# Writing out the loops over batches and over pairs of attention groups on every engine

## The chip, the cores and the metric

The kernel runs on one core of one Trainium2 chip. The metric is the device time of one execution in microseconds (us). Its engines are PE (matrix products; PEld is its weight load), DVE (vector), ACT (scalar), POOL (general) and SP, which here only issues transfers. Each runs its own list of instructions; they meet at semaphores.

## The reference, cut to what matters

Two transformer layers on x of (2, 1024, 1024), all in fp32: attention with rotary positions, a mixing layer, attention again, and an expert layer. The change touches the two attentions alone:

```python
x = x + _L0_attn_ref(_layernorm(x), wq, wk, wv, wo)   # 32 heads of 32, 8 key/value heads
x = x + _L0_ffn_ref(_layernorm(x), ...)
x = x + _L1_attn_ref(_layernorm(x), Wq, Wk, Wv, Wo)
x = x + _L1_ffn_ref(_layernorm(x), ...)

# in each attention, for batch b and key/value group g (4 query heads each):
scores = q @ k.T / sqrt(32), causal mask
attn = softmax(scores)
out = attn @ v
```

## The kernel before, in words

`attention` is built once for each layer. On every engine it has the same skeleton: some work for the first batch, then `batches` runs a function `batch` for the 2 batches, and inside it, after a prologue (the first projections), `over_groups` runs a function `group` for the 8 key/value groups. Groups 0 to 5 are three passes of a loop that executes on the engine (`eng.Fori`, L318) with two groups in its body, an even and an odd one; groups 6 and 7 are written out. `batches` has a loop too (L311), with a single pass for batch 0, while batch 1 is written out behind it. So there are 2 layers x 2 batches = 4 group loops on each engine, each with 3 passes and 2 taken branches back; "pair" below is one pass.

What a group does is set by hand in `ORDER` (`ORDER_7` for group 7), one list for all engines. `ST:e.h` is the transposed score product of unit e and head h on PE (L898), whose exponential ACT takes (L617). `S` are row scores of the next group (PE L851), whose maxima DVE takes (L710 with the mask, L713 without). `V` and `D` are the products with the values and with ones (L914, L927). `P:c.i` are pieces of the projection of a later group (L830), 24 products for one of two halves c. `MT` takes the larger of the two halves of the maxima (DVE L719), transposes them (PE L860) and sends them on. `NORM` is the division by the sum (DVE L758 to L764). `WS` prepares the weights of the next projection: ACT L590 takes the high part, POOL L463 the low one. Group 6 has the same list as 0 to 5 but for the projections (`P`, `WL`, `WS`, `RK`, `VG` and some more).

PE has a PSUM ring of three banks for `S` and `P` and another of three for `ST`; it waits for DVE (`sh_free`) or ACT (`exp_done`) until a bank is free again. Such a wait compares a semaphore, which only counts up, with a number like `SH0 + u + prev + 1`, where u depends on the batch and on the group. In the loop of L318 the group's number is in a register. So most waits in the loop's body compare with a register, and an instruction of the engine's own sequencer (REGISTER_ALU, or ISA, in the order below; ALU_OP or FUSED_REGOPS in a trace) computes it first. The batch's loop has one pass, and what depends on b is a constant already. Groups 6 and 7 and the prologue have constants throughout.

Of the kernel before, what the change touches and what calls it, by code (L numbers as in the profile page):

```python
# [22 lines left out]
B, S, D = 2, 1024, 1024  # L23
# [5 lines left out]
NG = 8  # L29
# [184 lines left out]
def attention(nc, sem, layer, x_in, wqkv, cos_in, sin_in, swap, oT_d):  # L214
# [37 lines left out]
    with ExitStack() as ctx:  # L252
# [55 lines left out]

        def batches(eng, batch):

            with eng.Fori(0, B - 1) as b:  # L311
                batch(b, False)
            batch(B - 1, True)

        def over_groups(b, eng, group, last):

            u0 = 1 + b * U_BATCH + U_PRO
            with eng.Fori(0, NG // 2 - 1) as j:  # L318
                for par in range(2):
                    group(bodies[par], b, j * 2 + par, j, par, u0 + (j * 2 + par) * U_IT)  # L320
            group(body6, b, NG - 2, NG // 2 - 1, 0, u0 + 6 * U_IT)
            group(body7 if last else ahead7, b, NG - 1, NG // 2 - 1, 1, u0 + 6 * U_IT + U_IT6)

        @block.sync
        def _(sp):
# [89 lines left out]
            def batch(b, last):  # L415

                sp.wait_ge(s["zT_ready"], ZT0 + (b + 1) * 2 * ST_)
                sp.sem_inc(s["sp_turn"], 1)
                def keys_and_queries(g):

                    if g == 0:
                        sp.wait_ge(s["k_out"], b * 64 + 32)
                        sp.sem_inc(s["sp_turn"], 1)
                        sp.wait_ge(s["st_ready"], ST0 + b * NG * NU * GH)
                        sp.sem_inc(s["sp_turn"], 1)
                    stack_keys(b, g, g)
                    for c in range(2 - g):
                        sp.wait_ge(s["q_lo"], b * RB + 2 * LO_ORDER.index((1, 4)[g]) + c + 1)
                        stack_queries(b * 2 * NG + g * 2 + c, g, c)

                load_w(b * N_WCHUNK + 2, 2, 0)
                store_k(b, 0)
                load_w(b * N_WCHUNK + 3, 3, 1)
                keys_and_queries(0)
                load_w(b * N_WCHUNK + 4, 4, 0)
                store_k(b, 1)
                load_w(b * N_WCHUNK + 5, 5, 1)
                load_w(b * N_WCHUNK + 6, 6, 0)
                keys_and_queries(1)
                load_w(b * N_WCHUNK + 7, 7, 1)  # L440
                sp.wait_ge(s["k_out"], b * 64 + 64)
                sp.sem_inc(s["sp_turn"], 1)
                row_max(b, 0, 0)
                over_groups(b, sp, group, last)

            batches(sp, batch)
            for qc in range(NQC):
                sp.wait_ge(o_stored[qc], DMA0 + 16 * B * NG)
# [5 lines left out]
        def _(pool):  # L454
# [98 lines left out]
            def batch(b, last):  # L553
                w_lo(b * N_WCHUNK + 1, 1)
                for step in pro:
                    what, p, *piece = step
                    if what == "P" and piece[1] == PIECES - 1:
                        c = piece[0]
                        i, _, _ = plan_pro[step[:-1]]
                        u = 1 + b * U_BATCH + i  # L560
                        if c == 0:
                            w_lo(b * N_WCHUNK + p + 1, (p + 1) % 2)
                        if p in VALUES:
                            pool.wait_ge(s["sh_free"], SH0 + u + 1)
                            pool.sem_inc(s["pool_turn"], 1)
                            pool.drain().then_inc(s["roped"], 1)
                        else:
                            turn_over(u, c)
                        if p in (1, 4) and c == 0:
                            part_lo(b * RB + 2 * LO_ORDER.index(p), 0)  # L570
                        if c == 1 and p in (0, 1, 2):
                            for h in range(p % 2, 2):
                                part_lo(b * RB + 2 * LO_ORDER.index(p) + h, h)
                    if what == "VT" and piece == [1]:
                        pool.wait_ge(s["v_ready"], b * 4 + 2 + 2 * VALUES.index(p))
                        pool.sem_inc(s["pool_turn"], 1)
                        if p == VALUES[0]:
                            copy_v(b, 0, 0)
                            copy_v(b, 1, 1)
                over_groups(b, pool, group, last)  # L580

            batches(pool, batch)

        @block.scalar
        def _(act):
# [66 lines left out]
            def batch(b, last):  # L652
                for p in range(6):
                    w_hi(b * N_WCHUNK + p + 1, b * 6 + (p + 1) // 2, (p + 1) % 2)
                    if p == 1:
                        act.wait_ge(s["k_out"], b * 64 + 32)
                    if p == 4:
                        act.wait_ge(s["k_out"], b * 64 + 64)
                    if p not in VALUES:
                        for c in range(2 if p < 4 else 1):  # L660
                            if p == 2:
                                act.wait_ge(s["q_out"], (b * 2 * NG + c + 1) * 32)
                            part_hi(b * N_WCHUNK + p, c)
                over_groups(b, act, group, last)

            batches(act, batch)

        @block.vector
# [1410 lines left out]
```

## Time and profile before

| | us |
|---|---|
| three timed runs | 2863.57, 2864.22, 2868.37 |
| median | 2864.22 |
| the profiled execution, its own time | 2866.59 |
| its span, first to last instruction | 2864.9 |
| PE busy | 2603.4 (91%) |
| DVE busy | 1780.9 (62%) |
| POOL busy | 1125.1 (39%) |
| ACT busy | 1094.2 (38%) |
| granted clock of PE, mean | 0.958 |

The profiled execution lies 2.37 us over the median, and 1.69 us of its own time lie outside its span. The two attentions take the stretches from the start to about 940 us and from about 1435 to 2390 us. The rest is the mixing layer between them, and the output projection and the expert layer at the end; those have loops of their own, which stay. Busy times of PE are modelled ends, since products overlap; an idle time counts only where the waits show one. Register, branch and semaphore instructions aren't counted as busy. In the views a lower-case q behind an engine's name stands for its sequencer, and "issue" as releaser is idle time for which the profile shows no one that was waited for.

### The profile page before, as it was taken

To read this page: it belongs to the slowest core of one execution; us is meant where nothing else is said; L and a number is where in the kernel's file an instruction comes from. 1 tells how busy PE (TensorE), PEld (TensorE's weight loads), DVE (VectorE), ACT (ScalarE), POOL (GpSimd) and SP (SyncE) were. 2 spreads that over 40 slices of the span, in tenths; PEclk is the share of its full clock that TensorE was granted. 3 is DMA by queue.
4 is the path that set the end of the run, shared out by engine and by line. 5 is a ranking of instruction groups with operands and counts; after the bars stand their busy time and mean duration, and the time that the engine had idled before them with its cause. 6 is when DMAs were issued, how large, how long until landed. Compare 5 with 4: busy or idle time off the path is not lost. (4 is left out here: it accounts for less than half of the span.)

```text
span 2864.9 us, 50928 instructions
## 1 busy us (share of the span) xinstructions
PE 2603.4 (91%) x15312; PEld 1826.8 (64%) x15312; DVE 1780.9 (62%) x4439; ACT 1094.2 (38%) x2381; POOL 1125.1 (39%) x801
## 2 busy tenths in 40 slices
PE   7999997999998799793979999989999996998999
PEld 6665654765654588682757566547656544886887
DVE  5677777567775433588756777775667763216443
ACT  2255454155555211372522454551454553002000
POOL 7466554556564100000063666546555642002110
PEclk9999999999999899896979999999999998999999
DMA  4323222432321421000243232224222314461211
GB/s 157 116 72 102 75 72 82 133 92 75 98 74 39 163 81 59 1 1 0 108 159 118 70 108 67 80 71 143 85 76 90 83 40 153 134 241 38 74 59 45
DMA packets 121076, 252.97 MB, mean 88 GB/s; under 512 B 12720, under 2 KB 39728, under 8 KB 120880
## 3 DMA queue, kind: packets, MB, share of 16 engines
q1 hardware_dynamic: 120912, 251.03, 27.4%
q8 instruction: 72, 1.18, 0.2%
q14 instruction: 92, 0.75, 0.1%
HBM read 166.57 MB, written 84.41 MB: 88 GB/s over the span
## 5 line engine op out<-in xcount | busy, mean ns | idle before, releaser
L617 ACT ACTIVATE a_prob<-a_pst 128x512 f32<-128x512 f32 (+3 forms) x1536 | 660.4, 494 | 535.5 <-PE a_pst L898 529.5
L710 DVE CUSTOM_DVE_ANT_0 a_psh<-a_psh,a_edge 128x128 f32<-128x128 f32 (+3 forms) x1024 | 480.0, 516 | 203.6 <-PE a_psh L851 182.7
L898 PE MATMUL a_pst<-a_qst,a_kst 128*128 128x512 f32 (+2 forms) x1536 | 487.6, 370 | 24.1 <-DMA a_qst<-rowmax 17.7
L517 POOL TENSOR_TENSOR a_prob<-a_prob 128x2048 f32<-128x2048 f32 (+1 forms) x96 | 405.9, 4228 | 245.6 <-PE a_ppv L914 230.0
L851 PE MATMUL a_psh<-a_kst,a_qst 127*128 127x512 f32 (+3 forms) x1536 | 485.3, 364 | 16.7 <-DVE a_mx L710 10.6
L851 PEld LDWEIGHTS a_psh<-a_kst,a_qst 127*128 127x128 f32 x1536 | 273.1, 190 | 230.7 <-DVE a_mx L713 92.7
L713 DVE TENSOR_REDUCE a_mx<-a_psh 128x1 f32<-128x512 f32 x512 | 329.1, 685 | 122.0 <-PE a_psh L851 120.9
L898 PEld LDWEIGHTS a_pst<-a_qst,a_kst 128*128 128x128 f32 x1536 | 286.2, 193 | 163.7 <-ACT a_prob L617 92.8
L914 PE MATMUL a_ppv<-a_prob,a_vg 128*32 128x512 f32 (+3 forms) x3072 | 321.8, 505 | 0.0
L502 POOL TENSOR_SCALAR_AFFINE_SELECT a_prob<-a_prob 128x512 f32<-128x512 f32 x256 | 162.2, 641 | 186.5 <-ACT a_prob L617 186.5
L927 PE MATMUL a_pden<-a_prob,a_ones 128*32 128x512 f32 (+3 forms) x2304 | 221.3, 474 | 9.0 <-POOL a_prob L517 9.0
L470 POOL TENSOR_TENSOR a_swp<-a_swp,a_sin 128x512 f32<-128x512 f32 x80 | 103.3, 1292 | 246.4 <-DVE a_swp L699 235.5
L830 PE MATMUL a_psh<-a_xT_hi,a_w_hi 128*128 128x512 f32 x416 | 170.7, 410 | 8.2 <-DVE a_vall L803 6.6
L1538 PE MATMUL h_pout<-h_w,h_o 128*128 128x512 f32 x720 | 167.7, 392 | 0.3 <-DVE h_x L1404 0.3
L830 PE MATMUL a_psh<-a_xT_hi,a_w_lo 128*128 128x512 f32 x416 | 165.5, 398 | 0.0
L830 PE MATMUL a_psh<-a_xT_lo,a_w_hi 128*128 128x512 f32 x416 | 165.1, 397 | 0.0
L1538 PEld LDWEIGHTS h_pout<-h_w,h_o 128*128 128x128 f32 x720 | 134.0, 188 | 28.2 <-issue 0.7
L830 PE MATMUL a_pst<-a_xT_hi,a_w_hi 128*128 128x512 f32 x352 | 139.6, 397 | 6.2 <-DVE a_swp L780 3.2
L710 DVE DVE_READ_ACCUMULATOR2_ANT a_mx<- 128x1 f32 x1024 | 143.0, 140 | 0.0
L914 PEld LDWEIGHTS a_ppv<-a_prob,a_vg 128*32 128x32 f32 x3072 | 71.9, 109 | 110.8 <-issue 66.4
L830 PE MATMUL a_pst<-a_xT_lo,a_w_hi 128*128 128x512 f32 x352 | 137.8, 392 | 0.0
L830 PE MATMUL a_pst<-a_xT_hi,a_w_lo 128*128 128x512 f32 x352 | 137.6, 391 | 0.0
(239 smaller groups left out, 4190.6 us busy)
## 6 DMA issues: line engine op xcount, KB each, us to landing
a_qst<-q SPq DMA_DIRECT2D x192, 256.0 KB, 4.4
a_wraw<-in_wqkv SPq DMA_DIRECT2D x52, 512.0 KB, 4.3
q<-a_stg_hi SPq DMA_DIRECT2D x64, 256.0 KB, 2.1
q<-a_stg_lo SPq DMA_DIRECT2D x64, 256.0 KB, 2.4
a_kst<-kT SPq DMA_DIRECT2D x96, 128.0 KB, 2.5
oT<-a_oT SPq DMA_DIRECT2D x32, 256.0 KB, 2.4
oT<-a_vT SPq DMA_DIRECT2D x32, 256.0 KB, 2.9
h_oraw<-oT SPq DMA_DIRECT2D x16, 512.0 KB, 4.0
```

The source lines that it names most:

```text
L470: pool.tensor_tensor(swp[c][:, :], swp[c][:, :], sin[:, c * BANK:(c + 1) * BANK], ALU.mult)
L502: pool.affine_select(out=blk, in_=blk, compare_op=ALU.is_ge, fill=0.0, base=0, pattern=[[0, GH], [1, P]], channel_multiplier=-1)\
L517: pool.tensor_tensor(into, into, prob[second % len(prob)][:, :, off:], ALU.add)\
L617: act.activation(prob[k % len(prob)][:, h, off:], pst[:, (k * GH + h) % 3, off:], ACT.Exp, scale=scale).then_inc(s["exp_done"], 1)
L710: part = dve.tensor_tensor_reduce(scores, scores, edge[:, BANK - n:], 1.0, 2 * MASKED, ALU.add, ALU.max, mx_hq[kc][:, h, qt:qt + 1])
L713: part = dve.tensor_reduce(mx_hq[kc][:, heads[0]:heads[0] + m, qt], psh[:, at, 0:m * n].rearrange("p (m n) -> p m n", n=n), AX.X, ALU.max)
L830: mm = pe.matmul(bank(at), w[par][a][:, k, :], xT[x][:, k, c * BANK:(c + 1) * BANK], start=(i == 0), stop=(i == len(passes) - 1))
L851: mm = pe.matmul(psh[:, at, i * n:(i + 1) * n], qst[par][0:P - 1, h, qt * P:(qt + 1) * P], kst[par][0:P - 1, kc * BANK:kc * BANK + n], sta ...
L898: pe.matmul(pst[:, (k * GH + h) % 3, off:], kst[par][:, ki * P:(ki + 1) * P], qst[par][:, h, qc * BANK + off:(qc + 1) * BANK], start=True, ...
L914: mm = pe.matmul(ppv[h * HD:(h + 1) * HD, off:], vg[par][:, ki, :], prob[k % len(prob)][:, h, off:], start=(ki == 0), stop=(ki == 4 * qc + ...
L927: mm = pe.matmul(pden[h * HD:(h + 1) * HD, off:], ones[:, :], prob[k[0] % len(prob)][:, h, off:], start=(ki == 0), stop=(UNITS[k[-1]][1] = ...
L1538: mm = pe.matmul(pout[:, half, :], o[:, par, a, k, :], w[:, b, k, half * BANK:(half + 1) * BANK], start=(i == 0), stop=(i == len(passes) - 1))
```

## The change

Both loops become loops of the program that builds the kernel, and each engine gets its passes written out one behind the other. `batches` calls `batch` for 0 and 1 and `over_groups` calls `group` for 0 to 5 with plain numbers. So in the two attentions the branches go, and so do the instructions that compute a wait's number or a transfer's address from a register. Every other instruction stays, in its order.

```diff
--- before.py
+++ after.py
@@ -308,14 +308,13 @@
 
         def batches(eng, batch):
 
-            with eng.Fori(0, B - 1) as b:
-                batch(b, False)
-            batch(B - 1, True)
+            for b in range(B):
+                batch(b, b == B - 1)
 
         def over_groups(b, eng, group, last):
 
             u0 = 1 + b * U_BATCH + U_PRO
-            with eng.Fori(0, NG // 2 - 1) as j:
+            for j in range(NG // 2 - 1):
                 for par in range(2):
                     group(bodies[par], b, j * 2 + par, j, par, u0 + (j * 2 + par) * U_IT)
             group(body6, b, NG - 2, NG // 2 - 1, 0, u0 + 6 * U_IT)
```

On DVE, this is how the loop of layer 0, batch 0 begins; its first row stands once ahead of the three passes, the second is the first of the body. ISA rows of L710 are a masked maximum and the reading of its result; L318 is the loop.

```order
L318 UNCONDITIONAL_BRANCH
L318 ISA
L710 ISA a_psh,a_mx<-a_psh,a_edge 128x128
L710 ISA a_mx 128x1
```

And this is how that body ends on DVE: the last projection's rotation, the division of the odd group, the branch.

```order
L694 REGISTER_ALU
L697 REGISTER_ALU
L698 TENSOR_TENSOR a_rots<-a_psh,a_cos 128x512
L699 STREAM_SHUFFLE a_swp<-a_psh 128x512
L755 REGISTER_ALU
L758 STREAM_TRANSPOSE a_vT<-a_dens 128x512
L760 RECIPROCAL a_rden<-a_vT 128x16
L762 STREAM_TRANSPOSE a_dens<-a_rden 128x512
L764 TENSOR_TENSOR a_vT<-a_pvs,a_dens 128x512
L318 REGISTER_ALU
L318 COMPARE_AND_BRANCH
```

In the changed kernel the same place on DVE, between groups 1 and 2, reads as follows (its lines stand one lower).

```order
L697 TENSOR_TENSOR a_rots<-a_psh,a_cos 128x512
L698 STREAM_SHUFFLE a_swp<-a_psh 128x512
L757 STREAM_TRANSPOSE a_vT<-a_dens 128x512
L759 RECIPROCAL a_rden<-a_vT 128x16
L761 STREAM_TRANSPOSE a_dens<-a_rden 128x512
L763 TENSOR_TENSOR a_vT<-a_pvs,a_dens 128x512
L709 ISA a_psh,a_mx<-a_psh,a_edge 128x128
L709 ISA a_mx 128x1
```

The maxima of group 2 now stand directly behind the division of group 1: the branch is gone, and so are the rows that computed numbers. Nothing else moved.

On ACT the start of the loop's body, in layer 0, batch 0, has one computed number for nearly every exponential.

```order
L318 ISA
L616 ISA
L617 ACTIVATE a_prob<-a_pst 128x512
L616 REGISTER_ALU
L617 ACTIVATE a_prob<-a_pst 128x512
L616 REGISTER_ALU
```

In the changed kernel ACT has there, at the same place, only the exponentials and the high part of the projection between them.

```order
L616 ACTIVATE a_prob<-a_pst 128x512 x4
L616 ACTIVATE a_prob<-a_pst 128x384 x3
L601 ACTIVATE a_stg_hi<-a_rots 128x512
L616 ACTIVATE a_prob<-a_pst 128x384
```

The work is the same and in the same order; the rows between it are gone.

## Rows read from the trace of the kernel before

**Rows 1.** page, part 1: engine, busy us (share) xinstructions.
```profile
span 2864.9 us, 50928 instructions
PE 2603.4 (91%) x15312; PEld 1826.8 (64%) x15312; DVE 1780.9 (62%) x4439; ACT 1094.2 (38%) x2381; POOL 1125.1 (39%) x801
```

**Rows 2.** busy time by stretch: us, PE, PEld, DVE, ACT, POOL, clock, DMA.
```profile
204.45:298.72 94.27, 92.38 (x626) 56.68 (x627) 70.57 (x192) 49.65 (x110) 56.83 (x38) 1.00 0.30 87
298.72:393.19 94.47, 92.45 (x627) 56.69 (x628) 70.57 (x192) 49.64 (x110) 56.82 (x38) 1.00 0.31 87
668.95:763.47 94.52, 92.35 (x627) 56.67 (x628) 70.56 (x192) 49.66 (x110) 56.80 (x38) 1.00 0.30 87
763.47:857.95 94.48, 92.35 (x626) 56.69 (x627) 70.54 (x192) 49.65 (x110) 56.80 (x38) 1.00 0.30 87
1642.80:1736.28 93.48, 92.13 (x626) 56.73 (x627) 70.50 (x192) 49.64 (x110) 56.83 (x38) 1.00 0.30 88
1736.28:1829.80 93.52, 92.19 (x626) 56.75 (x627) 70.49 (x192) 49.64 (x110) 56.84 (x38) 1.00 0.29 88
2102.85:2202.68 99.83, 94.80 (x627) 57.90 (x628) 70.78 (x192) 49.75 (x110) 56.85 (x38) 0.97 0.29 82
2202.68:2301.41 98.73, 93.91 (x626) 57.17 (x627) 70.69 (x192) 49.73 (x110) 56.85 (x38) 0.98 0.29 83
```

**Rows 3.** timeline, PE, 1736 to 1736.5: start, us, operation.
```profile
1736.28 0.28 PE L860 MATMUL a_psh<-a_ident,a_mx 128*32 128x128 f32 x1 [0.56 <-DVE a_mx L719]
```

**Rows 4.** waits: us in total, times, longest.
```profile
DVE a_psh L710 <- issue: 18.1, 8, 3.0
PE a_psh L860 <- DVE a_mx L719: 16.0, 28, 0.9
PE a_psh L851 <- DVE a_mx L710: 10.6, 6, 3.8
```

**Rows 5.** timeline, DVE, 2109.5 to 2122.
```profile
2110.34 1.18 DVE L764 TENSOR_TENSOR a_vT<-a_pvs,a_dens 128x512 f32<-128x512 f32 x1
2113.54 0.30 DVE L710 CUSTOM_DVE_ANT_0 a_psh<-a_psh,a_edge 128x128 f32<-128x128 f32 x1 [2.02 <-issue]
...
2117.36 0.30 DVE L710 CUSTOM_DVE_ANT_0 a_psh<-a_psh,a_edge 128x128 f32<-128x128 f32 x1 [2.96 <-issue]
```

**Rows 6.** timeline, DVE, 1650.2 to 1655.
```profile
1650.29 1.18 DVE L764 TENSOR_TENSOR a_vT<-a_pvs,a_dens 128x512 f32<-128x512 f32 x1
1651.39 0.29 DVE L710 CUSTOM_DVE_ANT_0 a_psh<-a_psh,a_edge 128x128 f32<-128x128 f32 x1
```

**Rows 7.** timeline, PE, 2111 to 2123.
```profile
2117.77 0.80 PE L851 MATMUL a_psh<-a_kst,a_qst 127*128 127x256 f32 x2 [3.81 <-DVE a_mx L710]
```

**Rows 8.** busy time by stretch, the two at half clock.
```profile
2116.20:2123.00 6.80, 5.23 (x21) 3.05 (x25) 3.91 (x15) 0.94 (x3) 1.45 (x2) 0.50 0.70 193
2218.60:2222.00 3.40, 3.40 (x17) 1.34 (x19) 2.30 (x9) 0.94 (x3) 1.27 (x1) 0.50 0.85 198
```

**Rows 9.** busy time by stretch: ST:8.0 to ST:10.3 in groups 1 and 6.
```profile
1627.28:1635.22 7.94, 7.94 (x47) 4.14 (x46) 6.11 (x15) 4.39 (x11) 5.32 (x4) 1.00 0.02 4
1860.26:1868.20 7.94, 7.94 (x47) 4.14 (x46) 6.11 (x15) 4.39 (x11) 5.24 (x4) 1.00 0.00 0
```

**Rows 10.** timeline, DVE and POOL, before the maxima's transposition.
```profile
1828.08 1.59 DVE L719 TENSOR_TENSOR a_mx<-a_mx 128x16 f32<-128x16 f32 x1 [0.18 <-issue]
...
1827.27 2.37 POOL L463 TENSOR_TENSOR a_w_lo<-a_wraw,a_w_hi 128x1024 fp32r<-128x1024 f32 x1 [0.35 <-ACT a_w_hi L590]
...
1872.69 0.17 DVE L719 TENSOR_TENSOR a_mx<-a_mx 128x16 f32<-128x16 f32 x1
```

**Rows 11.** DMA queues, 115.84 to 204.45: packets, MB, share of 16 engines.
```profile
q8 instruction: 6, 0.10, 0.5%
```

**Rows 12.** busy time by stretch, first ST to the transposition.
```profile
115.84:204.45 88.61, 87.24 (x605) 52.69 (x604) 63.85 (x180) 48.57 (x108) 53.50 (x35) 1.00 0.28 82
1647.75:1736.28 88.53, 87.19 (x605) 52.66 (x604) 66.74 (x185) 48.56 (x108) 56.83 (x38) 1.00 0.31 91
```

## The prediction, made before the changed kernel ran

> **What bounds the kernel now.** I first read the page's busy times: PE is busy for 91% of the span, the next engine, DVE, for 62% [rows 1]. Averages over stages with different limits prove little, so the second view is the busy time by stretch, cut at one mark that returns with every pair of groups: the transposition of the maxima on PE (L860), the last thing before the branch [rows 3]. There are eight such stretches, two behind each of the four group loops [rows 2]. Each holds the same 626 or 627 products, so they can be compared with each other. The reader should see three kinds. The two pairs of layer 1, batch 0 take 93.48 and 93.52 us, with PE busy 92.13 and 92.19 at a clock of 1.00: PE's own work bounds them. The four pairs of layer 0 take 94.27 to 94.52, at the same clock. The two of layer 1, batch 1 take 99.83 and 98.73, at 0.97 and 0.98. The same code on the same shapes should not take three different times.
>
> The third view, the waits, names the difference [rows 4]. PE waited 10.6 us in 6 waits for the masked maxima of DVE (L710), and DVE stood idle before those maxima for 18.1 us in 8 gaps which the profile puts down to "issue": it waited for nobody. Eight stretches, six of them long, and six waits of PE: they belong together. The timeline shows where. In the first pair of the last loop DVE's division L764 starts at 2110.34 and lasts 1.18 us, and the next maximum, the first thing behind the branch back, starts at 2113.54; after three more maxima comes a second hole of 2.96 us, until 2117.36 [rows 5]. In layer 1, batch 0, at the same place, the maximum starts 1.10 us after the division does, 1651.39 against 1650.29, and there is no hole [rows 6]. So a taken branch costs DVE some 2 to 3 us of its time in six cases of eight, and in two of these the code behind it stops DVE a second time. I read it as DVE fetching its instructions again: the body is long, and where its pieces lie in the instruction memory is another in each of the four copies. PE has little in reserve at this point, since its PSUM ring is three banks deep. [...]
>
> **The change part by part.** It removes from the attentions all taken branches (8 on each engine), and the instructions that compute numbers for waits and addresses. It adds no work, wait or queue entry and moves none past another; it adds only code that has to be fetched.
>
> *The branches.* The reference is the mean of the two undisturbed pairs, (93.48 + 93.52) / 2 = 93.50 [rows 2]. Layer 0: 94.27 + 94.47 + 94.52 + 94.48 = 377.74, less 4 x 93.50 = 374.00, is 3.74 us. Layer 1, batch 1: 99.83 + 98.73 = 198.56, less 187.00, is 11.56 us. This second sum can be split by the same rows: the idle time of PE is 5.03 and 4.82 there against 1.34 in a clean pair, together 7.17 more, and the busy time is 94.80 and 93.91 against 92.16, together 4.39 more, which is the half clock. In layer 1, batch 0 nothing is to be had. Sum: 15.30 us. When the hole goes, what is late next is nothing new: a clean pair already runs with 1.33 to 1.35 us of idle PE.
>
> [...]
>
> *The computed numbers.* They are cheap to bound, because group 6 runs the same list with constants. From product ST:8.0 to ST:10.3, a stretch without projections in both, group 1 (registers) takes 7.94 us and group 6 (constants) 7.94 us, with PE busy throughout [rows 9]. So they hide behind PE's work and I take zero. The upper end: the one wait of PE that remains in a pair is for the transposition, 16.0 us in 28 waits [rows 4], 24 of them in the loops at 0.56 [rows 3], 13.4 us. It would be gained only if DVE's L719 came earlier. But L719 lasts 1.59 us in the loop and 0.17 in group 6; it starts at 1828.08, 0.81 us behind the weight preparation of POOL, which runs from 1827.27 to 1829.64, and ends with it, at 1829.67 [rows 10]. One computed number fewer ahead of it is part of a gap of 0.18 us; it would have to be 0.81 earlier. POOL's start hangs on ACT and so on PE. I take zero, and keep 13.4 as the end of the gain. A loss from fewer instructions I bound at zero too, but for the fetching below.
>
> *The longer code.* Today the second and third pass fetch nothing on PE; the first pass does, 6 packets of code [rows 11]. With everything written out all passes fetch like the first. The first pass of layer 0, batch 0, from its first ST to the transposition, takes 88.61 us; the second of layer 1, batch 0, with its code in place, takes 88.53 [rows 12]. So straight code streams in at a price of 0.08 us at most per pass. Eight passes become such: 0.6 us, within what two equal passes differ by; I take zero. The other end: a late fetch is worth as much as a branch today, and the rival below counts it. No gap of DVE before L710 lies elsewhere: six branches and the two second holes make up all eight [rows 4].
>
> Stages outside the attentions keep their code and their loops. Their code lies elsewhere in memory, but loops with much shorter bodies show no such idle time in the waits, so I expect no change there.
>
> **The sum.** 2866.59, the profiled execution's own time, less 15.30 is 2851.3. It stood 2.37 us over the median of the runs, so for the median I say 2864.2 - 15.3 = 2848.9, about 2849 us.
>
> **The rivals.**
> *The computed numbers matter too.* Each engine's sequencer has less to do, DVE answers earlier, and the wait at the transposition shrinks. For it speaks that nearly every wait in the loop has one such instruction in front; against it the equal 7.94 [rows 9]. With half of 13.4 it is 2842, with all of it 2835.5.
> *The half clock stays.* PE's clock may fall at these places for another reason than the hole, and only the idle time goes. Then of 15.3 the 4.4 of the slow products stay: 2853.3. For it speaks that other stretches without a hole fall too, since the mean is 0.958; against it that in the loops both falls stand right behind the two longest stalls of PE, and the six cleaner pairs have 1.00 [rows 2, 8].
> *The holes move and the end doesn't.* If DVE's hole only takes time that PE then loses at the transposition, the time is that of before, 2864. Against it: the clean pairs have the same wait there, 0.56 [rows 3], and are shorter.
> *Straight code arrives late: slower.* Place: PE, at each new piece of its code, in the eight passes that fetch none today. At the first pass's rate of 6 that is 48 pieces. Price: a packet keeps a DMA engine busy for 0.005 x 16 x 88.6 / 6 = 1.2 us [rows 11], and a piece that comes too late holds PE for at least that; all 48 make 57 us, so 2906. It decides from 13 late pieces on, where it eats the 15.3. Against it stands the first pass, which fetched 6 and lost 0.08 [rows 12].
> That the change doesn't do what it says is excluded: in the order of the changed kernel the branches and the computed numbers are gone.
>
> **How the numbers follow.** The forecast as worked out (2845 to 2853) gets 0.70, the first rival 0.10, the second 0.11, the third 0.05, the fourth 0.04. What a measurement of this kernel can tell from no change is about 0.2%, 5.7 us: faster means below 2858.5, slower above 2869.9. The forecast and the first two rivals lie below; the third is the same; the fourth is mostly slower. That gives faster 0.90, same 0.06, slower 0.04. For the range I take the forecast's own bounds and go down to 2840, which holds the half of the first rival, and up to 2857, which holds the second rival and a run like the slowest of the three, 4 us over the median.
>
> **What the changed profile would show.** Right: "DVE L710 <- issue" and "PE L851 <- DVE L710" all but gone; every pair from transposition to transposition at 93.5 us, in layer 1, batch 1 too, at a clock of 1.00; PE's wait at the transposition unchanged at 0.56; more packets of code on the queue that PE's come by. Wrong: pairs well under 93.4 would show that the computed numbers cost something; a pair that stays above 94 without a gap on DVE, that the holes were not the cause; gaps with the releaser "issue" on PE or DVE in the middle of a group, that straight code comes late.

## The result, and the profile after

The written-out kernel takes 2850.95 us (median of 5 runs, 2849.54 to 2854.61), the kernel before 2867.75 in the same comparison: ratio 0.9946, 95% interval 0.9936 to 0.9957. Forecast were 2849.0 us and a gain of 15.3; the medians differ by 16.8, the profiled executions (2866.59 and 2849.54) by 17.05. The size is right. The places are right only in part, as the stretches show. Lines of the kernel after are one lower than before: L859 is the transposition of the maxima (L860 before), L850 the row scores, L709 the masked maxima.

The page after, parts 1 and 3, and its line of code packets in the kernel before below it:

```profile
span 2847.4 us, 44980 instructions
PE 2593.4 (91%) x15312; PEld 1821.4 (64%) x15312; DVE 1783.5 (63%) x4439; ACT 1093.3 (38%) x2381; POOL 1123.5 (39%) x801
q8 instruction: 108, 1.77, 0.3%
q14 instruction: 86, 0.70, 0.1%
```

```profile
q8 instruction: 72, 1.18, 0.2%
q14 instruction: 92, 0.75, 0.1%
```

PE is busy 10.0 us less than in [rows 1] with the same 15312 products. The mean granted clock is 0.964 over the span, where the kernel before had 0.958; since the clock is either 1.00 or 0.50, that is 206 us of 2847.4 at half speed against 242 of 2864.9. 5948 instructions fewer ran (44980 against 50928), and queue 8 has 36 packets more, 108 against 72. I call queue 8 that of PE's code, since its count follows PE's loops alone: 108 in all five kernels of this study with PE written out, 72 in the nine others. Queue 14 follows the other engines: 92 packets before, 92 with PE alone written out, 86 with all but PE, 76 with DVE alone.

After, the eight pairs of groups from transposition to transposition, as in [rows 2], and the first of the two stretches over group 6 in layer 0, then that of layer 1 (columns as in [rows 2]):

```profile
202.87:296.21 93.34, 92.08 (x626) 56.75 (x626) 70.89 (x192) 49.62 (x110) 56.72 (x38) 1.00 0.30 89
296.21:389.83 93.62, 92.07 (x627) 56.74 (x628) 70.80 (x192) 49.69 (x110) 56.73 (x38) 1.00 0.30 89
666.06:760.52 94.46, 92.13 (x627) 56.75 (x627) 70.98 (x192) 49.72 (x110) 56.75 (x38) 1.00 0.30 88
760.52:854.19 93.67, 92.32 (x627) 56.74 (x628) 70.44 (x192) 49.61 (x110) 56.71 (x38) 1.00 0.30 89
1636.84:1730.35 93.51, 92.06 (x627) 56.74 (x628) 70.85 (x192) 49.62 (x110) 56.71 (x38) 1.00 0.31 89
1730.35:1823.77 93.42, 92.03 (x626) 56.74 (x627) 70.80 (x192) 49.61 (x110) 56.71 (x38) 1.00 0.31 89
2096.86:2191.00 94.14, 92.14 (x626) 56.73 (x626) 70.91 (x192) 49.61 (x110) 56.72 (x38) 1.00 0.31 88
2191.00:2284.34 93.34, 92.09 (x627) 56.76 (x628) 70.82 (x192) 49.53 (x110) 56.74 (x38) 1.00 0.30 89
389.83:436.39 46.56, 42.34 (x280) 23.17 (x281) 32.39 (x93) 23.15 (x53) 22.07 (x15) 0.96 0.14 41
1823.77:1867.06 43.29, 40.95 (x281) 22.51 (x281) 32.20 (x93) 23.05 (x53) 22.06 (x15) 1.00 0.15 44
```

The kernel before at the two group-6 stretches of layer 0:

```profile
393.19:437.08 43.89, 42.55 (x280) 23.03 (x281) 32.12 (x93) 23.20 (x53) 22.07 (x15) 0.96 0.15 44
857.95:901.35 43.40, 40.97 (x281) 22.52 (x281) 32.12 (x93) 23.16 (x53) 22.07 (x15) 1.00 0.15 44
```

The eight pairs now add up to 749.50 us, against 763.30 in [rows 2]: 13.80 less. Every clock is 1.00. But group 6 of layer 0 is longer, 46.56 against 43.89, and in batch 1 (854.19 to 900.48) 46.29 against 43.40: 5.56 us given back. As a result the last instruction of layer 0's attention starts at 945.0 us, where it started at 944.75 before: nothing is left of its gain. The attention of layer 1, from DVE's first instruction in it to the start of the last one, went from 948.5 to 934.7 us. The sum of all is 17.5 us of span: +0.25 up to the end of layer 0's attention, -3.33 in the mixing stage, -13.75 in layer 1's attention, -0.67 behind it.

The waits after, with the one of before that answers to the last row below them (columns as in [rows 4]):

```profile
PE a_psh L859 <- DVE a_mx L718: 13.7, 28, 0.6
PE a_psh L850 <- DMA a_qst<-q: 12.7, 16, 2.8
```

```profile
PE a_psh L851 <- DMA a_qst<-q: 3.5, 7, 1.3
```

Both waits of DVE's holes are gone from the list, "DVE L710 <- issue" (18.1) and "PE L851 <- DVE L710" (10.6) of [rows 4]. The timeline of DVE after, at the branch's old place in layer 1, batch 1, against [rows 5]:

```profile
2104.18 1.25 DVE L763 TENSOR_TENSOR a_vT<-a_pvs,a_dens 128x512 f32<-128x512 f32 x1
2105.35 0.29 DVE L709 CUSTOM_DVE_ANT_0 a_psh<-a_psh,a_edge 128x128 f32<-128x128 f32 x1
```

The maximum starts 1.17 us after the division, as in [rows 6], where it was 3.20 in [rows 5]. What took their place is a wait for a transfer: PE at the row scores (L850) for the second half of the next group's queries, 12.7 us in 16 waits. The longest is in group 6 of layer 0:

```profile
411.60 0.79 PE L850 MATMUL a_psh<-a_kst,a_qst 127*128 127x512 f32 x1 [2.80 <-DMA a_qst<-q]
```

SyncE's queue shows why it is late. First the kernel before, group 6 of layer 0, batch 0: two stores of the queries' parts, then the three transfers that stack them.

```profile
404.54 0.33 SPq L342 DMA_DIRECT2D q<-a_stg_hi  x1
404.92 0.43 SPq L342 DMA_DIRECT2D q<-a_stg_lo  x1
407.31 1.28 SPq L345 DMA_DIRECT2D a_qst<-q  x3
```

And after:

```profile
401.09 0.33 SPq L341 DMA_DIRECT2D q<-a_stg_hi  x1
401.46 0.43 SPq L341 DMA_DIRECT2D q<-a_stg_lo  x1
405.88 1.56 SPq L344 DMA_DIRECT2D a_qst<-q  x3
```

The stacking waits for the stores to land. From the second store it took 2.39 us before and takes 4.42 after. The DMA view of these few microseconds (KB each, median us from issue to landing) follows, first before (403 to 410), where it has no line of queue 8, as no packet of that queue starts between 201.2 and 411.9, then after (400.5 to 409), where it has one:

```profile
q<-a_stg_lo SPq DMA_DIRECT2D x1, 256.0 KB, 2.4
```

```profile
q8 instruction: 1, 0.02, 0.7%
q<-a_stg_lo SPq DMA_DIRECT2D x1, 256.0 KB, 4.4
```

A packet of PE's code, 16384 bytes in 0.96 us, starts at 403.4, while the store is under way, and the store lands 2.0 us later than it did before. PE then waits 2.80 us, and its clock is at half from 411.3 to 414.7 (0.96 over the stretch). The kernel before has a half-clock stretch of 3.4 us in this step too, from 402.7, right behind a wait of 0.67 us for ACT (until 402.44); such a wait doesn't decide it, since group 6 of layer 0, batch 1 has one of 0.46 us there and keeps the full clock, and the same group in the run `e8_starts_14_22_1_124` further down has one of 0.68 us and keeps it too.

The theory that I took to the experiments, H: the gain is DVE's refetch after taken branches alone; PE's written-out code gives part of it back, by packets that meet the store of the queries. The rivals were that group 6 is late because it is reached earlier (A), and that the other engines' constants and branches made part of the gain (B, C).

### The profile page after: what moved, and what is told of

Same layout as the page of the kernel before. It is cut to its first block and busy times, and to the rows that moved or that the text cites. A ratio compares the mean times of both kernels' runs of the same rounds, so it can differ in the third digit from the quotient of the medians.

```text
span 2847.4 us, 44980 instructions
## 1 busy us (share of the span) xinstructions
PE 2593.4 (91%) x15312; PEld 1821.4 (64%) x15312; DVE 1783.5 (63%) x4439; ACT 1093.3 (38%) x2381; POOL 1123.5 (39%) x801
## 5 line engine op out<-in xcount | busy, mean ns | idle before, releaser
L709 DVE CUSTOM_DVE_ANT_0 a_psh<-a_psh,a_edge 128x128 f32<-128x128 f32 (+3 forms) x1024 | 479.9, 515 | 183.3 <-PE a_psh L850 180.3
L850 PE MATMUL a_psh<-a_kst,a_qst 127*128 127x512 f32 (+3 forms) x1536 | 484.4, 363 | 14.5 <-DMA a_qst<-q 12.7
L850 PEld LDWEIGHTS a_psh<-a_kst,a_qst 127*128 127x128 f32 x1536 | 272.9, 189 | 226.1 <-DVE a_mx L712 92.4
L709 DVE DVE_READ_ACCUMULATOR2_ANT a_mx<- 128x1 f32 x1024 | 143.0, 140 | 0.0
```

The costliest lines, as they stand in the source:

```text
L709: part = dve.tensor_tensor_reduce(scores, scores, edge[:, BANK - n:], 1.0, 2 * MASKED, ALU.add, ALU.max, mx_hq[kc][:, h, qt:qt + 1])
L850: mm = pe.matmul(psh[:, at, i * n:(i + 1) * n], qst[par][0:P - 1, h, qt * P:(qt + 1) * P], kst[par][0:P - 1, kc * BANK:kc * BANK + n], sta ...
```

## Experiments: whose loops matter

The group and batch loops were chosen by engine (this edit serves the next four runs, with another tuple in each):

```diff
+WRITTEN = (mybir.EngineType.DVE,)
         def batches(eng, batch):
+            if eng.engine in WRITTEN:
+                for b in range(B):
+                    batch(b, b == B - 1)
+                return
             with eng.Fori(0, B - 1) as b:
...
+            if eng.engine in WRITTEN:
+                for j in range(NG // 2 - 1):
+                    pair(j)
+            else:
+                with eng.Fori(0, NG // 2 - 1) as j:
+                    pair(j)
```

**DVE alone written out.**

> Only VectorE's loops are written out; SyncE, GpSimd, ScalarE and TensorE keep theirs and their computed semaphore values. Theory H (the gain is VectorE's refetch after a taken branch, and the written-out code of TensorE gives 5.6 us back, because its code packets delay the query transfers of group 6 in layer 0): the segment from ST:0.0 to ST:4.0 is 11.3 us in every loop group, the step from MT to MT over group 6 of layer 0 goes back from 46.4 to about 43.8 us, the time is about 2845.5 us, ratio 0.9925 to the kernel before. Rival A (group 6 is slow because it is now reached earlier, whatever TensorE's code does): group 6 stays 46.4 us, 2851 us, ratio 0.9945. Rival B (constants on the other four engines made part of the gain): under half of it comes, 2857 us or more.

Measured: 2846.11 us, ratio 0.9938 (0.9925 to 0.9952). The pairs add up to 747.4 us and group 6 of layer 0 is short:

```profile
391.78:435.20 43.42, 40.98 (x281) 22.50 (x281) 32.21 (x93) 23.26 (x53) 22.06 (x15) 1.00 0.15 44
853.10:896.34 43.24, 40.95 (x281) 22.52 (x281) 32.21 (x93) 23.16 (x53) 22.07 (x15) 1.00 0.15 44
```

H and its number held. One engine of five, with registers and loops left on the other four, gives the whole gain. It is also the fastest kernel of the study, though its interval overlaps that of the kernel with everything written out.

**All but PE written out.**

> All engines but TensorE are written out; TensorE keeps its two loops, so its queue fetches its loop body once in each layer and batch. Theory H: TensorE's code packets go back to about those of the kernel before (72 on its queue), group 6 of layer 0 goes back to about 43.8 us, 2845.5 us, ratio 0.9925. Rival A: group 6 stays at 46.4 us, 2851 us. Rival C (TensorE's own constants gain something): 2853 us or more, since TensorE computes its numbers again.

Measured: 2849.9 us, ratio 0.9946 (0.9932 to 0.9959), with 72 packets on queue 8. Group 6 of layer 0 takes 43.46 and 43.26 us, so rival A falls: it is reached early here too. The total missed H's number (2845.5) by 4 us. Against the kernel after, group 6 won 6.1 us and the pairs 1.9, but the four first passes (transposition 0 to 2) take 389.95 us against 386.92, and the ways from batch 0 to batch 1 3.3 us more. So part of what H promised went elsewhere; I come back to this.

**All but DVE written out.**

> All engines but VectorE are written out; VectorE keeps its loops, so its taken branches stay. Theory H: the holes of 2.8 and 3.0 us stay at the same six jumps, and TensorE's code packets are there: 2866 to 2872 us, ratio 1.000 to 1.002. Rival B (constants and branches of the other engines made part of the gain): 2855 to 2860 us. Rival D (a hole follows any jump in step with the other engines' own refetch): the holes go, 2850 us.

Measured: 2867.69 us, ratio 1.0007 (0.9997 to 1.0016). The holes are at the same jumps; DVE in layer 1, batch 1:

```profile
2111.70 1.18 DVE L776 TENSOR_TENSOR a_vT<-a_pvs,a_dens 128x512 f32<-128x512 f32 x1
2114.90 0.30 DVE L722 CUSTOM_DVE_ANT_0 a_psh<-a_psh,a_edge 128x128 f32<-128x128 f32 x1 [2.02 <-issue]
...
2118.21 0.30 DVE L722 CUSTOM_DVE_ANT_0 a_psh<-a_psh,a_edge 128x128 f32<-128x128 f32 x1 [2.45 <-issue]
```

Four engines written out bring nothing. Rivals B and D fall.

**PE alone written out.**

> Only TensorE's loops are written out. Theory H: about the time of the kernel before, or up to 5.6 us more if its code packets delay the query transfers: 2866 to 2872 us, ratio 1.000 to 1.002; code packets of TensorE's queue rise from 72 to 108; the second stacking of queries in a group starts late (11.1 us after ST:0.0 and more, where 10.4 is usual) in the groups in which a code packet falls beside the queries' store. Rival A (code packets have no part in the late queries): the stacking is on time as in the kernel before, 2866 us, ratio 1.000. Rival C (TensorE's constants gain): below 2860 us.

Measured: 2866.67 us, ratio 1.0004 (0.9995 to 1.0013). Group 6 of layer 0 takes 46.55 and 44.73 us, and its stacking starts 11.53 and 11.27 us after ST:0.0, where the kernel before has 10.16 and 9.81. So PE's code alone makes the queries late. The second is 1.8 us shorter though it is only 0.26 us less late. There PE's half-clock stretch lies at 866.6 to 870.0, ahead of the wait, which is 0.82 us where the first has 2.53. I read it so that PE, slowed before, comes later to the late queries; lateness alone doesn't set the price. Rival C, below 2860 us by PE's constants, falls.

## Experiments: where PE's code packets fall

**The written-out kernel with PE's code moved by 128 instructions.**

```diff
+            if layer == 0:
+                for _ in range(128):
+                    pe.sem_inc(s["pe_turn"], 1)
             pe.wait_ge(s["const"], 1)
```

> The changed kernel (all engines written out); TensorE executes 128 semaphore increments more at the start of layer 0, where it waits for the first tile, so that its code packets (one for 256 instructions) come half a packet's distance, about 9 us, earlier or later in the same work. Theory H (in group 6 of layer 0 a code packet that falls between the store and the stacking of the queries makes the stacking 1.8 us late, and TensorE waits at the second half of the row scores): the packets at 403.4 and 867.2 us are now near 394 and 413, 858 and 878 us, the stacking of these groups is back at 9.8 us after ST:0.0, the step over group 6 from MT to MT goes from 46.56 and 46.29 to 43.4 us, 2845.5 us, ratio 0.9925. Rival (the written-out kernel's group 6 is late for another reason): 46.4 us stay, 2851 us, ratio 0.9945.

Measured: 2859.54 us, ratio 0.9979 (0.997 to 0.9988). The increments cost 0.153 us each and weren't hidden, as I had assumed they would be: the first transposition of the maxima comes at 119.31 us instead of 106.85. Behind it the forecast came true, since the two stretches over group 6 are short:

```profile
402.91:446.41 43.50, 40.97 (x281) 22.52 (x281) 32.19 (x93) 23.15 (x53) 22.05 (x15) 1.00 0.15 44
864.44:907.70 43.26, 40.93 (x281) 22.50 (x281) 32.19 (x93) 23.06 (x53) 22.05 (x15) 1.00 0.15 44
```

The time less the 12.46 us of delay is 2859.54 - 12.46 = 2847.1, where 2845.5 was expected and the kernel after has 2850.95. Same instructions behind the start, same constants: only the place of the packets differs.

**The same with 88, at places where PE waits.** The 128 became 40 ahead of the first transpose and 12 behind each of the first four tiles'.

> The changed kernel; TensorE executes 88 semaphore increments more in layer 0, at 0.153 us each, 40 before the first transpose, 12 behind each of the first four tiles' transposes, where it waits anyway, so that the shift of its code packets costs no time of its own. Theory H: the packets of group 6 of layer 0 fall some 6 us from where they were (403.4 and 867.2 us), before the queries are stored; the step over group 6 is 43.4 us in both batches; time 2845 us, ratio 0.9925 to 0.993, below the changed kernel by 5 to 6 us. Rival (something of the 128 increments' effect was theirs and not the packets'): group 6 stays at 46.4 us, 2851 us, ratio 0.9945.

Measured: 2855.72 us, ratio 0.9968 (0.9957 to 0.998). The padding was nearly free (first transposition at 107.57 us, 0.7 later than in the kernel after), group 6 of layer 0 became short (43.68 and 43.22), and the number was still missed by 10 us: now layer 1 pays.

```profile
1824.15:1870.83 46.68, 42.51 (x281) 22.90 (x281) 32.34 (x93) 23.27 (x53) 22.07 (x15) 0.96 0.14 41
2285.88:2332.30 46.42, 42.41 (x280) 23.18 (x280) 32.41 (x93) 23.26 (x53) 22.07 (x15) 0.96 0.14 41
```

That confirms that such packets and late landings go together and refutes my use of it: the shift moves all packets behind it. The rest is in layer 0: the step ahead of group 6 in batch 1 takes 48.75 us where 46.82 was, and the way from batch 0 to batch 1 3.8 us more. Eight runs (before, after, both shifts and the four by engine) hold 32 groups 6. In 8 of them a packet of queue 8 starts 8.1 to 9.2 us after ST:0.0, right behind the second store (7.2 to 7.6). In these 8 the stacking follows the store by 3.75 to 4.42 us; in the other 24, with packets elsewhere or none, by 2.36 to 2.58. The six runs with padding on DVE add 24 groups 6 without such a packet, at 2.36 to 2.47. Why a packet of 1 us holds the store up for 2, no view shows, and outside group 6 the rule is looser: in two groups of the loops a packet 1.9 to 2.0 us behind the store changed nothing (the stacking followed by 2.38 in both), and some stores there land late with no packet of queue 8 near, as the one at 678.64 in the run with 17 increments on DVE, after 3.9 us.

## Experiments: why only some copies of DVE's loop had holes

All of DVE's loop copies hold 367 instructions; the trace of the kernel before has as many of DVE's from one taken branch (2110.44) to the next (2210.27). Theory P: DVE's code comes in blocks of 128, and a body stays in place when it touches three of them. The 128 is an estimate from packet sizes: in the kernel after, 8953 instructions of PE start in the 35 intervals between queue 8's packets from 215.3 to 935.6, which is a packet of 16384 bytes for 256 of them on average, or 64 bytes for each, and at this rate queue 14's packets of 8192 bytes are 128 instructions. The edit is the same throughout, with four numbers:

```diff
+DVE_PAD = ((99, 17), (12, 17))
...
+                for _ in range(DVE_PAD[layer][int(last)]):
+                    dve.sem_inc(s["dve_turn"], 1)
                 over_groups(b, dve, group, last)
```

> The kernel before with all its loops; VectorE executes 99, 17, 12 and 17 semaphore increments more, just ahead of its four group loops, so that each loop body (367 instructions) starts at the same place in a block of 128 instructions as the one of layer 1, batch 0, which had no hole. Theory P (the room for VectorE's code is a few blocks of 128 instructions: a body that touches three blocks stays, one that touches four is fetched again at each taken branch): no hole after any branch, ST:0.0 to ST:4.0 is 11.3 us in all loop groups, group 6 of layer 0 takes 43.4 us, time 2845 to 2848 us, ratio 0.993, as with VectorE alone written out. Rival Q (the holes have to do with the length of the body or with what other engines fetch, not with where it starts): holes of 2.8 us stay at the same jumps, 2865 us, ratio 1.000.

Measured: 2858.32 us, ratio 0.998 (0.9971 to 0.9989). Half right: layer 1 has no hole in either batch, layer 0 has one at each jump. Its first pair and that of layer 1, batch 1:

```profile
206.59:302.03 95.44, 92.43 (x626) 56.71 (x627) 70.23 (x192) 49.62 (x110) 56.73 (x38) 1.00 0.29 86
2103.45:2196.75 93.30, 92.10 (x626) 56.76 (x627) 70.49 (x192) 49.63 (x110) 56.77 (x38) 1.00 0.30 88
```

> The kernel before with all its loops; VectorE executes 17 semaphore increments more ahead of its first group loop, which moves all four bodies by 17 instructions: the one of layer 1, batch 1 now starts where that of layer 1, batch 0 did, and that one 17 further on, 24 into a block. Theory P: the holes of layer 1, batch 1 go (pairs from 99.8 and 98.7 to 93.5 us, the half clock behind them too), and layer 1, batch 0 gets one after each taken branch (pairs 93.5 to 94 up to 99, by what hides them), those of layer 0 stay: 2853 to 2866 us, ratio 0.996 to 1.000. Rival Q: the holes stay in layer 1, batch 1 and none come in batch 0: 2865 us, ratio 1.000.

Measured: 2855.83 us, ratio 0.9971 (0.9958 to 0.9984). The holes changed places: layer 1, batch 1 is free (93.28 and 93.22 us), layer 1, batch 0, the only copy without them before, has them:

```profile
1640.92:1735.62 94.70, 92.35 (x627) 56.66 (x627) 70.19 (x192) 49.65 (x110) 56.77 (x38) 1.00 0.30 87
2104.58:2197.86 93.28, 92.15 (x626) 56.74 (x627) 70.47 (x192) 49.64 (x110) 56.78 (x38) 1.00 0.30 88
```

Rival Q falls: 17 increments that compute nothing move the fault from one loop to the other.

> The kernel before with all its loops; VectorE executes 106, 25, 119 and 12 semaphore increments more ahead of its four group loops. By the count of instructions, with the start of layer 1, batch 0 in the kernel before taken as 7 into a block of 128, the bodies now start 14, 22, 1 and 124 into a block. Theory P (367 instructions from a start up to 17 touch three blocks, from a later one four): no hole in layer 0, batch 0; one of about 2.8 us after each taken branch in layer 0, batch 1; none in layer 1, batch 0; holes in layer 1, batch 1 as in the kernel before, with the second of each pair about four instructions behind the branch's target. Rival Q: no such pattern.

One run, 2875.96 us. Layer 1 as expected: none in batch 0, two in batch 1, and both now lie ahead of the first maximum, by theory P because the end of the block moved with the start, from the ninth instruction behind the jump to the third:

```profile
2119.32 1.19 DVE L765 TENSOR_TENSOR a_vT<-a_pvs,a_dens 128x512 f32<-128x512 f32 x1
2126.08 0.30 DVE L711 CUSTOM_DVE_ANT_0 a_psh<-a_psh,a_edge 128x128 f32<-128x128 f32 x1 [5.57 <-issue]
```

That is the second hole of [rows 5] joined to the first. Layer 0, batch 0 missed: holes again. So I looked for layer 0's offset.

> The kernel before with all its loops; VectorE executes 35, 35, 68 and 18 semaphore increments more ahead of its four group loops. Theory P says, with layer 1's places counted from the two copies whose holes are known: the bodies of layer 1 start 17 and 18 into a block of 128; 367 instructions from 17 end with the third block, from 18 they need a fourth, so batch 0 has no hole and batch 1 has one of about 2.8 us after each of its taken branches. Layer 0's count is open, since all starts tried there had holes: if it is offset from layer 1's by instructions that I don't count, the free stretch of 18 starts lies elsewhere, and these two starts (22 and 40 by the program's own count modulo 128) cover 36 of the 64 places that are left. Rival Q (layer 0 has holes wherever it starts): holes in both batches of layer 0 here and in the next run.

One run, 2867.89 us. All four copies have holes; the bound of 17 in layer 1 was missed. The first jump there:

```profile
1658.50 0.30 DVE L711 CUSTOM_DVE_ANT_0 a_psh<-a_psh,a_edge 128x128 f32<-128x128 f32 x1 [3.00 <-issue]
```

> The kernel before with all its loops; VectorE executes 71, 29, 21 and 16 semaphore increments more ahead of its four group loops. Theory P: the bodies of layer 1 start 0 and 127 into a block of 128, so batch 0 has no hole and batch 1 has one after each taken branch (and a second one within two instructions, if at all apart). Layer 0: starts 58 and 70 by the program's count, the other places that are left; by theory P at least one of the four copies of layer 0 in this and the run before has no hole. Rival Q: all four have.

One run, 2858.20 us. Layer 0, batch 1 and both batches of layer 1 are free; layer 0, batch 0 now has two holes, as layer 1, batch 1 had before, with the half clock too:

```profile
204.59:304.86 100.27, 95.01 (x626) 57.91 (x627) 70.81 (x192) 49.70 (x110) 56.78 (x38) 0.97 0.28 82
679.66:773.19 93.53, 92.13 (x627) 56.79 (x628) 70.52 (x192) 49.63 (x110) 56.77 (x38) 1.00 0.29 88
```

I fix the count by it, reading a second hole as the end of a block (it stands at the 9th instruction behind the jump in the two pairs here and in the two of layer 1, batch 1 in the kernel before, at the 3rd in the two of `e8_starts_14_22_1_124`): my places of layer 1 were 2 too low, and layer 0 stands 11 further on. Counted so, all 28 copies of the loop, in the kernel before and the six with padding on DVE, fall in line (a hole is given from the start of one instruction to that of the next, the branch and register instructions counted, which the timelines above leave out):

```
start within a block of 128     at the jump
1, 2, 3, 4, 9                   no hole
19, 20                          one of 3.4 to 3.6 us
26 to 102 (eight starts)        one of 2.8 to 3.1 us
120                             one of 2.8 to 3.0, a second of 3.0 to 3.2 us at the 9th instruction
126                             one of 2.8 to 3.0, a second of 3.7 us at the 3rd instruction
```

If the blocks are of 128, 367 instructions end inside the third from a start up to 17, as 17 + 367 = 3 x 128; the runs show no hole up to 9 and one from 19 on, and nothing between was tried. The period of 128 can be read from layer 1: in the run with 99, 17, 12 and 17 its batch 0 stands 128 instructions further on than in the kernel before and is free again, and its batch 1 stands 145 further on and is free as well as with 17. How many blocks DVE has room for beyond the three, no run shows. The offsets of 2 and 11 were fitted to these same runs; what tests them is the next run, whose layer 0 was set by them. The miss in the run before is explained by this count, since its 17 and 18 were 19 and 20. That layer 1, batch 1 counted as 127 is free, where a hole was expected, is too: it was 1.

That a hole is a refetch, the code packets of queue 14 show. Over the two pairs of layer 1, batch 1 in the kernel before (2102.85 to 2301.41), and over those of layer 1, batch 0 in the run with 17 increments (1640.92 to 1830.19), its line in the DMA view is

```profile
q14 instruction: 10, 0.08, 0.1%
```

and over the pairs of the other batch in each (1642.80 to 1829.80; 2104.58 to 2291.08) the queue has no packet at all. So it is in all 28 copies: 10 packets in the 16 that have holes, five for each taken branch, none in the 12 that have none. In the first hole of [rows 5] such a packet runs from 2111.46 to 2111.93, between the branch at 2110.44 and the next instruction at 2113.27.

**All four loops put right.** The numbers are 83, 17, 22, 17.

> The kernel before with all its loops; VectorE executes 83, 17, 22 and 17 semaphore increments more ahead of its four group loops. By the places found in the runs before, where the count of layer 0 stands 11 instructions off that of layer 1, all four bodies now start 2 or 3 instructions into a block of 128 and touch three blocks. Theory P: no hole after any taken branch in either layer, all twelve loop groups of a layer at 46.6 to 46.7 us but the first, group 6 at 43.4 us; the time is that of the kernel with layer 1 alone put right (2858.3 us) less the four pairs of layer 0 at 95.3 that become 93.4: 2850.7 us, ratio 0.995. Rival: layer 0 keeps holes of 2.8 us and more, 2858 us or above, ratio 0.998.

Measured: 2849.48 us, ratio 0.9949 (0.9935 to 0.9962). No hole in either layer, and the pairs are:

```profile
205.65:299.00 93.35, 92.14 (x627) 56.80 (x628) 70.58 (x192) 49.64 (x110) 56.75 (x38) 1.00 0.29 88
299.00:392.35 93.35, 92.13 (x626) 56.82 (x627) 70.58 (x192) 49.63 (x110) 56.73 (x38) 1.00 0.30 88
```

With every loop kept and no code less, 139 idle instructions give the gain of writing all of it out.

## Why the prediction was right

*The branches, 15.30 us.* Shown, and as a refetch. The pairs lost 13.80; in layer 1, batch 1 they went from 198.56 to 187.48, 11.08 where 11.56 was forecast, in layer 0 from 377.74 to 375.09, 2.65 where 3.74 was. With DVE alone written out the pairs lost 15.9. What kept the kernel after from it is in part the late queries: PE waits 1.2 us for them in the pair of 94.46 and 1.1 us in that of 94.14.

*The half clock goes with the holes.* Right: 1.00 in all eight. Two details of the reading were off. The second hole of [rows 5] comes after three maxima, not after three more behind the first. And in the first pair the clock doesn't fall behind PE's long wait but within it: PE stands still from 2113.96 to 2117.77, and the half clock starts at 2116.2. In the second the wait ends at 2217.48, and the half clock starts at 2218.6. The rival that it stays falls, and the other way round, the run that gave layer 0, batch 0 two holes gave it the half clock.

*The computed numbers, zero.* Nearly right. The wait at the transposition is 15.5 to 16.0 us in the kernels that keep PE's loops (before, DVE alone, all but PE, all aligned: 16.0, 15.6, 15.5, 15.7) and 13.7 to 14.2 where PE is written out. So PE's constants, or its missing branches, which no run separates, shorten this wait by about 2 us of the 13.4 that I named as the upper end, and those of the other engines by nothing that shows.

*The longer code, zero.* This step failed. I asked whether PE would wait for its own code, found 0.08 us at most in a first pass [rows 12], and made "straight code arrives late" the only rival. PE's code did arrive in time: before, no packet of queue 8 starts in the second and third pass of layer 0, batch 0 (204.45 to 393.19), after, 10 do (202.87 to 389.83), and six of the eight pairs take 93.34 to 93.67 us, the two longer ones with a wait for queries in them; the four first passes take 386.9 us, not more than the 392.2 before. What I left out is that its packets travel beside the data: a packet that meets the queries' store costs 1.4 to 2.0 us of landing in group 6, and PE stood still for it. The term is +5.56 us, in layer 0 only by the accident of where the packets fell. A bound from first passes could hardly show it, because the groups with a projection lose less at this point: in the run with all but DVE written out three of them have a store that lands after 3.9 to 4.1 us beside a packet, and PE waits 0.5 to 0.7 us there, against 2.6 and 2.9 in its two late groups 6.

*Other stages, zero.* That shorter loops have no such hole holds in the waits of the kernel before: outside the attentions DVE's longest wait for "issue" is 0.9 us (L1509, 56 times). The mixing stage was 2.9 us shorter without being touched. Before, and after:

```profile
953.18:1431.81 478.63, 401.20 (x2048) 344.38 (x2048) 295.76 (x603) 179.79 (x431) 11.73 (x17) 0.92 0.17 59
```

```profile
953.40:1429.11 475.71, 398.81 (x2048) 342.68 (x2048) 295.80 (x603) 179.60 (x431) 11.68 (x17) 0.92 0.17 59
```

Of it 2.39 us is PE's busy time on the same 2048 products, which goes with the half clock: 81.0 us of it in the first stretch, 75.7 in the second. The kernel with DVE alone written out spends 479.35 us there and is faster all the same. From PE's first to its last product of this stage thirteen of the fourteen kernels take 471.0 to 474.7 us and one 479.5, though none touches it, and the kernel after happens to be the shortest. I take it as chance between programs, not as the change's doing; no run isolates it.

*The rest.* The four first passes went from 392.2 to 386.9 us. They are 385.9 to 387.1 in the five kernels with PE written out, and 387.8 or more in the nine that keep PE's loops. So some of this gain, 5.3 us here, comes from PE's side, and it offsets group 6. Why is open; I had it nowhere in the sum. The 17.5 us of span are -13.80 in the pairs, -5.30 in the first passes, -3.33 between the two attentions, most of it the mixing stage, +5.56 in group 6 of layer 0 and -0.6 in all the rest. One term of these was forecast. That the total agrees as well as it does is in part luck: the three that I had at zero are -5.30, -3.33 and +5.56, and add up to only -3.1.

## What to carry to other kernels

When copies of one loop take different times, look at the first instructions behind the backward jump on each engine, and before writing out everything write out the one engine that has a hole there: here one of five gave 0.9938, all five 0.9946, the other four 1.0007. If the code must stay short, move the loop's start instead; that costs some idle instructions (139 here), and has to be done again after every edit ahead of it, since 17 instructions there were enough to move the holes. Count the code packets of a long straight program as transfers, and look which small store with a waiter behind it they meet.

## What was not expected of the hardware

- A hole can be moved from one loop to another by 17 instructions that do nothing; a pair gets 0.6 to 3.4 us longer than 93.50 by one hole and 4.6 to 6.8 by two. Each pair with two holes had 3.4 or 6.8 us at half clock as well; of those with one only the longest had it (3.4 us). Each taken branch with a hole brings five code packets, one without brings none.
- A store of 256 KB that lands in 2.4 us took 3.7 to 4.4 in the 8 groups 6 in which one 16 KB code packet, itself 0.9 to 1.5 us long, started within 2 us of its issue.
- A semaphore increment on PE takes 0.153 us when 128 stand in a row, 19.6 us together.
